# Second stage's first rows and query weights prepared in the last tiles of the first stage, on a new layout of buffers

## What is computed

```
# layer 0, and the attention of layer 1: cross attention over 77 context rows, 16 heads of 32
q, k, v = x @ Wq.T + bq, ctx @ Wk.T + bk, ctx @ Wv.T + bv
a = softmax((q k^T * tau + delta) / sqrt(32)); x = x + (a v) @ Wo.T + bo
# layer 0, feed forward on the normalized row
s = ln(x) @ Win + bin; x = x + (sum_h relu(s * W1 + b1) * W2 + b2) @ Wout + bout
# layer 1, feed forward: local attention over windows of 64 rows and both neighbours, 8 heads of 64
q, k, v = split(ln_w(x) @ Wqkv.T); light = softmax(q k_window^T / 8) v_window @ Wout_l.T
# and routing: 50 iterations on one score per row, top 256 / 512 rows of each sequence,
# dense attention among the chosen rows, scattered back
```

## Time and profile before

| | us |
|---|---|
| median of 3 runs (lowest, highest) | 3143.72 (3143.63, 3144.43) |
| the profiled execution's own time | 3161.28 |
| its span, first to last instruction | 3159.4 |
| mean granted TensorE clock | 0.975 of full speed |
| TensorE, VectorE, GpSimd, ScalarE busy | 2985.1, 2378.9, 1780.1, 1540.8 |

### The profile page before, as it was taken

One profiled execution on the slowest core, in us unless ns is written; L12 is line 12 of the kernel. 1 busy time (PEld: TensorE's weight loads), 2 busy tenths in 40 slices (PEclk: granted clock), 3 DMA queues, 4 the chain that ended last, 5 costly groups with the idle time before them and its releaser, 6 DMA issues.

```text
span 3159.4 us, 58477 instructions
## 1 busy us (share of the span) xinstructions
PE 2985.1 (94%) x24002; PEld 2324.6 (74%) x24002; DVE 2378.9 (75%) x3974; ACT 1540.8 (49%) x2349; POOL 1780.1 (56%) x1284
## 2 busy tenths in 40 slices
PE   7999999999999999999969999999999999979898
PEld 4777777777677777777747777777777777857776
DVE  4788888888888988888746767778878775566453
ACT  2566666666666666565433434333333333334343
POOL 1666565656558999999834545454455445573210
PEclk9999999999999999999979999999999999999999
DMA  4001010101112111111120111111222221131100
GB/s 161 34 30 54 28 56 29 55 34 55 46 54 83 51 57 51 54 41 41 64 84 27 57 54 59 59 56 53 66 91 87 74 77 61 47 134 54 34 18 11
DMA packets 87466, 180.42 MB, mean 57 GB/s; under 512 B 9526, under 2 KB 10294, under 8 KB 85664
## 3 DMA queue, kind: packets, MB, share of 16 engines
q1 hardware_dynamic: 82512, 161.73, 14.6%
q0 software_dynamic: 3968, 10.50, 1.1%
q10 hardware_dynamic: 720, 4.46, 0.3%
HBM read 106.05 MB, written 70.60 MB: 56 GB/s over the span
## 4 chain that ended last, share of the span: by engine, by line
PE 77%; DVE 11%; POOL 4%; issue 4%; ACT 3%; DMA 1%; POOLq 0%; SPq 0%; another core or an unknown queue 0%; DVEq 0%; ACTq 0%
PE ps L264 17%; PE ps L266 15%; PE ps L265 15%; PE ps L271 7%; PE ps L259 4%; PE ps L1129 4%; PE ps L479 3%; PE ps L491 3%; PE ps L1149 3%; PE ps L500 2%; PE ps L1723 2%; DVE Sb L636 1%; DVE sTa L616 1%; POOL sTa L842 1%; PE ps L1706 1%
## 5 line engine op out<-in xcount | busy, mean ns | idle before, releaser
L822 POOL TENSOR_TENSOR Sb<-Sb,mx 128x1232 f32<-128x1232 f32 x128 | 295.9, 2312 | 158.4 <-DVE mx L643 158.4
L827 POOL TENSOR_TENSOR Sb<-Sb,dn 128x1232 f32<-128x1232 f32 x128 | 288.6, 2254 | 155.9 <-DVE dn L651 155.7
L1536 POOL TENSOR_TENSOR Sw<-Sw,dw 128x1024 f32<-128x1024 f32 x128 | 242.3, 1894 | 233.1 <-DVE dw L1254 232.8
L1481 ACT COPY PU<-ps 128x512 f32<-128x512 f32 x256 | 141.1, 588 | 438.2 <-PE ps L271 437.2
L777 ACT COPY PT<-ps 77x1024 f32<-77x1024 f32 x256 | 256.8, 1003 | 181.3 <-PE ps L491 179.7
L1531 POOL TENSOR_TENSOR Sw<-Sw,mw 128x1024 f32<-128x1024 f32 x128 | 243.3, 1901 | 121.7 <-DVE mw L1247 121.6
L1241 DVE TENSOR_TENSOR Sw<-ps,msk 128x1024 f32<-128x1024 f32 x128 | 155.6, 1216 | 105.2 <-PE ps L1129 105.2
L271 PE MATMUL ps<-ident,xn 128*128 128x128 f32 x1120 | 176.0, 285 | 55.4 <-ACT xn L709 15.4
L264 PE MATMUL ps<-Wo,OTp 128*128 128x512 f32 x512 | 208.7, 408 | 19.5 <-DVE OTp L655 19.0
L636 DVE TENSOR_TENSOR Sb<-ps,dlt 128x616 f32<-128x616 f32 x256 | 198.3, 775 | 37.4 <-PE ps L479 37.3
L479 PE MATMUL ps<-KB,QT 64*128 64x154 f32 x2048 | 198.0, 314 | 26.1 <-DVE Sb L636 25.9
(11 more groups left out here) (276 smaller groups left out, 8135.0 us busy)
## 6 DMA issues: line engine op xcount, KB each, us to landing
XB<-in_x SPq DMA_DIRECT2D x16, 1024.0 KB, 5.5
x_scratch<-XB SPq DMA_DIRECT2D x16, 1024.0 KB, 4.4
XB<-x_scratch SPq DMA_DIRECT2D x16, 1024.0 KB, 5.7
x_scratch<-XB SPq DMA_DIRECT2D x64, 256.0 KB, 2.0
XL<-x_scratch SPq DMA_DIRECT2D x64, 256.0 KB, 3.0
XY<-x_scratch SPq DMA_DIRECT2D x64, 256.0 KB, 2.7
y_scratch<-XY SPq DMA_DIRECT2D x64, 256.0 KB, 2.0
out<-yo SPq DMA_DIRECT2D x64, 256.0 KB
```

The costliest lines, as they stand in the source:

```text
L822: G.tensor_tensor(sv, sv, last(mx[:, n % 2, :], NK), ALU.subtract).then_inc(g_sub, 1)
L827: G.tensor_tensor(sv, sv, last(dn[:, n % 2, :], NK), ALU.mult).then_inc(g_norm, 1)
L1536: G.tensor_tensor(weights(n, p), weights(n, p), last(dw[:, n % 2, 4 * p:4 * p + 4], 256), ALU.mult).then_inc(bg_norm, 1)
```

## The change

- **Layout.** Three arenas now outlive the stages. Wq moves into `arena_q`; the second stage's split query weights WlQ lie on it, and later XH, the gathered rows. XB moves into `arena_b`; on it lie QU, PU, XL (on the slot that unit 27 used, LASTB = 3) and Wlo[0], later xh and KH. On `arena_x`, beside raw, lie KU (on raw), route (on raw's last part), nulq, XY and yo. Wl becomes WlQ, WK and WV, each [128, 4, 512] in two halves.
- **Rows.** `early`, at place 12200 of the first stage, has SyncE load the first four tiles into XL once unit 27 is stored and scored; the four loads at the second stage's head go.
- **Raw weights.** `raws` loads three column parts (query, key, value; 1 MB each) on three semaphores in place of four row parts.
- **Query weights.** `wq`, at 12650, 12670, 12690, 12710, splits them in the first stage: four scaled copies on ScalarE, four fused subtractions on VectorE (128 x 512).
- **Second stage's head.** The split is twelve pieces of 128 x 512 at new places: key weights -306 to -297, value weights -296 to -287, output weights -266 to -257. The null query row is loaded by `loadn` at -150, after the value weights' split.
- **Waits.** Key copies (ScalarE) and the first routing step (VectorE) wait for the value weights' split. The gathers at the stage's end wait for the last query group (b_qk 124), no longer for the last key and value groups.

```diff
+LASTB = (2 * NB - 4) % 5
     yield 400 * (2 * NB - 1) + 100, "raws", ()
+    yield 400 * (2 * NB - 1) - 200, "early", ()
+    for k in range(4):
+        yield 400 * (2 * NB - 1) + 250 + 20 * k, "wq", (k,)
...
-    for k in range(8):
-        yield -300 + 3 * k, "wl", (k,)
+    for k in range(12):
+        yield -306 + (0, 10, 40)[k // 4] + 3 * (k % 4), "wl", (k,)
...
+    yield -150, "loadn", ()
...
-        QU, Sw = at("QU", 0, [128, 2, 4, D]), at("Sw", 4096, [128, 2, 2048])
+        KU, XY = at("KU", 0, [128, 2, 4, 640]), at("XY", 6144, [128, 3, D])
...
+        at_q, at_b = arena("arena_q", 4096), arena("arena_b", 10240)
+        Wq = [at_q(f"Wq{i}", 2048 * i, [128, 4, D], R) for i in (0, 1)]
+        WlQ = [at_q(f"Wlq{i}", 2048 * i, [128, 4, D], R) for i in (0, 1)]
+        XB = at_b("XB", 0, [128, 5, 4, D])
+        QU, PU = at_b("QU", 0, [128, 2, 4, D]), at_b("PU", 4096, [128, 16, 128])
+        XL = at_b("XL", 2048 * LASTB, [128, 4, D])
...
@@ first stage, VectorE
+            def wq(k):
+                ve.wait_ge(a_whi, 21 + k)
+                V.scalar_tensor_tensor(WlQ[1][:, k, :], raw[:, k, 0:D], lnwb[:, k:k + 1], WlQ[0][:, k, :].bitcast(F),
+                                       ALU.mult, ALU.subtract).then_inc(v_wlo, 1)
@@ first stage, ScalarE
+            def wq(k):
+                ac.wait_ge(pe_q, 8 * NB)
+                ac.wait_ge(ld_raw[0], 16)
+                ac.wait_ge(ld_small, 144)
+                A.mul(WlQ[0][:, k, :], raw[:, k, 0:D], lnwb[:, k:k + 1]).then_inc(a_whi, 1)
@@ first stage, SyncE
-                for k in range(4):
-                    SY.dma_start(raw[:, k, :], a["wqkv"][:, k, :]).then_inc(ld_raw, 16)
+                for p in range(3):
+                    SY.dma_start(raw[:, :, D * p:D * p + D], a["wqkv"][:, :, D * p:D * p + D]).then_inc(ld_raw[p], 16)
+
+            def early():
+                done_x(2 * NB - 5)
+                for n in range(4):
+                    SY.dma_start(XL[:, n, :], X3d[128 * n:128 * n + 128, :]).then_inc(ld_xl[n], 16)
...
@@ second stage, TensorE
-                pe.wait_ge(bv_wl, 4)
+                if k < 4:
+                    pe.wait_ge(v_wlo, 24)
+                else:
+                    pe.wait_ge(bv_wl, 4)
...
@@ second stage, VectorE (the split; ScalarE's half is cut in the same way)
             def wl(k):
                 ve.wait_ge(ba_wl, k + 1)
+                w, j = (WK, WV, Wlo)[k // 4], k % 4
+                if k < 8:
+                    q = slice(D * (k // 4 + 1), D * (k // 4 + 2))
+                    V.scalar_tensor_tensor(w[1][:, j, :], raw[:, j, q], lnwb[:, j:j + 1], w[0][:, j, :].bitcast(F),
+                                           ALU.mult, ALU.subtract).then_inc(bv_wl, 1)
...
@@ the gathers, GpSimd
             gp.wait_ge(bv_rt, 42)
-            gp.wait_ge(b_qk, 8 * NB)
-            gp.wait_ge(b_v, 68)
+            gp.wait_ge(b_qk, 8 * (NB - 1) + 4)
...
@@ key copies, ScalarE
                     c = k - 4
+                    ac.wait_ge(bv_wl, 8)
...
@@ second stage, SyncE
+            def loadn():
+                sy.wait_ge(bv_wl, 8)
+                SY.dma_start(nulq[:, :], a["nulq"]).then_inc(ld_nq, 16)
...
-            for n in range(4):
-                load_xl(n)
             SY.dma_start(wlo_raw, a["wlo"]).then_inc(ld_w2, 16)
             SY.dma_start(msk[:, :, :], a["c_mask"]).then_inc(ld_w2, 16)
-            SY.dma_start(nulq[:, :], a["nulq"]).then_inc(ld_w2, 16)
```

More of the change, by code:

```diff
@@ L308, in build @@
         vepsl, nm_, rs = sb("vepsl", [128, 2, 4]), sb("nm_", [128, 2, 4]), sb("rs", [128, 2, 4])
-        Wq = [sb(f"Wq{i}", [128, 4, D], R) for i in (0, 1)]
         Wo = [sb(f"Wo{i}", [128, 4, D], R) for i in (0, 1)]
@@ L522, in wbias @@
                     p = take("wbo")
+                    pe.wait_ge(ld_raw[2], 16)
                     pe.wait_ge(g_cf, 4)
@@ L969, in sync_a @@
             block(2)
-            walk_a(vals0=vals0, vals1=vals1, loadk=loadk, loadv=loadv, store=store, storeb=storeb, kv=kv, loadx=loadx, wlo=wlo, raws=raws)
+            walk_a(vals0=vals0, vals1=vals1, loadk=loadk, loadv=loadv, store=store, storeb=storeb, kv=kv, loadx=loadx, wlo=wlo, raws=raws, early=early)
             for i in range(4):
@@ L980, in build @@
         pa.close()
-        at = arena("arena_w", 12288)
-        Wl = [at(f"Wl{i}", 6144 * i, [128, 4, 3 * D], R) for i in (0, 1)]
+        at = arena("arena_w", 8192)
+        WK, WV = ([at(f"Wl{n}{i}", 2048 * i + o, [128, 4, D], R) for i in (0, 1)] for n, o in (("k", 0), ("v", 4096)))
         places = (("Wkv", 0, 2 * D), ("Wh", 4096, D), ("Who", 6144, D))
@@ L996, in build @@
         xU = [sb(f"xU{i}", [128, 4, 576], R) for i in (0, 1)]
-        Wlo = [sb(f"Wlo{i}", [128, 4, D], R) for i in (0, 1)]
+        Wlo = [at_b("Wlo0", 8192, [128, 4, D], R), sb("Wlo1", [128, 4, D], R)]
         msk = sb("msk", [128, 3, 256])
-        nulq = sb("nulq", [128, D])
-        XL = sb("XL", [128, 4, D])
-        XY = sb("XY", [128, 3, D])
-        KU = sb("KU", [128, 2, 4, 640])
+        nulq = at_x("nulq", 5632, [128, D])
+        Sw = sb("Sw", [128, 2, 2048])
         VU = sb("VU", [128, 10, D])
-        PU = sb("PU", [128, 16, 128])
         wlo_raw = PU[:, :, :].rearrange("p a b -> p (a b)").rearrange("p (k m) -> p k m", k=4)
         mw, dw = sb("mw", [128, 2, 8]), sb("dw", [128, 2, 8])
-        yo = sb("yo", [128, D])
-        rout = sb("route", [128, 4, 128])
+        yo = at_x("yo", 7680, [128, D])
+        rout = at_x("route", 5120, [128, 4, 128])
         sr, zr, er = rout[:, 0, :], rout[:, 1, :], rout[:, 2, :]
@@ L1114, in v @@
                 pe.wait_ge(bv_xlo, 4 * i + 4)
-                pe.wait_ge(bv_wl, 4)
+                pe.wait_ge(bv_wl, 8)
                 r = 128 if j < 4 else 64
                 q = slice(128 * j, 128 * j + r)
-                mms3(ps[0:r, p, :], [(xU[0][:, x, q], xU[1][:, x, q], Wl[0][:, x, 2 * D:3 * D],
-                                      Wl[1][:, x, 2 * D:3 * D]) for x in range(4)]).then_inc(b_v, 1)
+                mms3(ps[0:r, p, :], [(xU[0][:, x, q], xU[1][:, x, q], WV[0][:, x, :], WV[1][:, x, :])
+                                     for x in range(4)]).then_inc(b_v, 1)
             def scores(n, p):
@@ L1469, in wl @@
             def wl(k):
-                if k < 4:
-                    ac.wait_ge(ld_raw, 64)
-                    A.mul(Wl[0][:, k, :], raw[:, k, :], lnwb[:, k:k + 1]).then_inc(ba_wl, 1)
-                else:
-                    ac.wait_ge(ld_w2, 80)
-                    A.copy(Wlo[0][:, k - 4, :], wlo_raw[:, k - 4, :]).then_inc(ba_wl, 1)
+                w, j = (WK, WV, Wlo)[k // 4], k % 4
+                if k < 8:
+                    ac.wait_ge(ld_raw[k // 4 + 1], 16)
+                    q = slice(D * (k // 4 + 1), D * (k // 4 + 2))
+                    A.mul(w[0][:, j, :], raw[:, j, q], lnwb[:, j:j + 1]).then_inc(ba_wl, 1)
+                else:
+                    ac.wait_ge(ld_w2, 64)
+                    A.copy(w[0][:, j, :], wlo_raw[:, j, :]).then_inc(ba_wl, 1)
             def pcopy(n, q):
@@ L1614, in build @@
         yg = sb("yg", [128, 3, 2, D])
-        xh = [sb(f"xh{i}", [128, 4, 768], R) for i in (0, 1)]
-        QH, KH = sb("QH", [128, 2, 4, 256]), sb("KH", [128, 2, 4, 512])
+        xh = [at_b(f"xh{i}", 3072 * i, [128, 4, 768], R) for i in (0, 1)]
+        QH, KH = sb("QH", [128, 2, 4, 256]), at_b("KH", 6144, [128, 2, 4, 512])
         VH = sb("VH", [128, 2, 4, 8, 65])
```

44 lines of the change are left out of this document (21 added, 23 removed).

## The result

The changed kernel took 3130.41 us (median of 5 runs, 3124.34 to 3132.15) where the kernel before took 3143.82 in the same comparison (5 runs, 3143.63 to 3146.01): 13.4 us faster by the medians. The ratio of the means is 0.9952 [0.9938, 0.9967], 0.48% or 15 us. The forecast was 3135.5, the range 3132.5 to 3140.5: the direction was right, the gain larger than the range allowed. Two repeats in later comparisons gave 0.9969 [0.9957, 0.9980] and 0.9966 [0.9954, 0.9978]; the three, weighted by their intervals, give 0.9964, some 11 us.

The account below looks back on a forecast made before the run. TensorE was taken as the bound, busy 94% of the span, so only its standing stretches could give time. Head 7.15, gate 1.0 and last tiles 0 gave 3143.7 - 8.2 = 3135.5 us, 8-in-10 range 3132.5 to 3140.5.

Parts of the forecast that it names:

- Head of the second stage: Seam of first and second stage: first query matmul at 1626.5 instead of 1633.65 us, 9.7 us after the last reduction.
- The half microsecond for the memset: Second stage's head: GpSimd's edge clearing holds the first normalization, ending it at 1618.1 instead of 1617.5 us.
- the 7.15 us: Second stage's head: term 1, queries start 7.15 us earlier and the gain is carried on; between 5.0 and 7.65.
- the 1.7 us that I had put in play there: Second stage's first queries: the same first 4.4 us at 1.2 GHz assumed, with some 1.7 us in play.
- Rival 3: Second stage's queries: clock does not rise, nine more matmul groups at 1.2 GHz cost 18.4 us, time 3153.9; chance 0.03.
- Last tiles: End of first stage: query weights' split costs zero under TensorE's work; likely 4.1 us on VectorE against 9.5 idle.
- Gate: End of second stage: first gather starts at 2778.2 instead of 2781.03 us, gated by the last query group.
- term 2: End of second stage, GpSimd's chain: 1.0 us gained from the earlier gathers, between 0 and 2.8.
- 7.15 + 1.0 + 0 = 8.2: Whole kernel: second stage's head, gathers' gate and first stage's last tiles summed; 8.2 us subtracted from the 3143.7 us median.

Follow-up runs that it names:

- rep_after: The changed kernel run again with nothing altered; 3149.58 us, ratio 0.9969 to the kernel before.
- the hole: Third stage's last gather burst held until TensorE turned 25 half tiles: kernel before 3154.49 and 3150.47 us, changed kernel 3143.89 and 3136.91 us.
- gate_back: The changed kernel with only the gathers' gate as before (last key and value group in place of last query group); ratio 0.9980 to the kernel before.
- hole_after: The changed kernel with the third stage's last gather burst held until TensorE turned 25 half tiles; 3143.89 us, ratio 0.9955 to the kernel before.

## Why the prediction was right and wrong

**Head of the second stage: right, term by term.** Gap 9.09, 9.31 and 9.08 us in three profiles of the changed kernel (9.7 predicted), against 16.85 and 16.38. The rows' part was 3.5 us and the query split's 2.4, and the order's 1.5. The half microsecond for the memset was too much: three normalizations took 1.52 to 1.53 us, in rep_after 1.68, so it held them by 0.15 us at most. What VectorE showed in the earlier trace rows beside a 4160-wide memset does not carry over to two of 256.

**What the clock gave back.** I carried the 7.15 us to the end unchanged. From the last reduction to the stage's first output sum the kernel before takes 88.4 to 88.7 us (four profiles, those with the hole counted in, since it lies behind), the changed schedule 81.4 to 82.5 (six): 6.4, not 7.4. gate_back has the same head and took 79.9, so the six don't show the whole spread. The stretch between the first query matmul and that sum holds the difference: 12.6 to 13.0 us of it are at the lower clock in five of the six (9.8 in the first profile, 5.6 in gate_back) and 8.1 to 8.7 in the kernel before. The level rose 5.8 to 6.2 us into the queries in the five, 4.6 to 5.3 before; the greater part is a second fall, 44 us in, which lasted 6.8 us instead of 3.4. Of the 1.7 us that I had put in play there, 1 was lost, but mostly at a fall that I hadn't looked at. Rival 3 did not come: the level rose.

**Last tiles: right that they cost nothing.** The hold came (6.15 us for four, L628's sort), and VectorE's idle time took it: TensorE stood no longer than without it, 8.1 us. Doubled, 1.9 us showed. Here I named a rule of the Trainium skill, SBUF — State Buffer, Who interferes with whom, by which a VectorE instruction with two SBUF inputs contends with a GpSimd instruction that reads SBUF. The trace agrees: 2.10 us beside GpSimd's 2.25, 0.66 without. In five other profiles with the split in that place the four took 3.0 to 3.4 us, so the hold is a matter of where they fall.

**Gate: right in the first profile, mostly absent in the later ones.** 1.3 us at the subtraction, and 0.1 to 0.2 in the eight later profiles, since ScalarE's late start takes the wait's place: the lower bound of my term 2. Over the stretch from the 56th to the 64th output sum, nine profiles with the new gate took 115.8 to 116.7 us and nine with the old one 115.9 to 119.2, means 116.2 and 117.2: 1.0, but that is where the clock fell: all nine with the new gate have 3.4 us at the lower clock there, and the four old ones that also have 3.4 took 115.9 to 116.9. Whether the gate moves the clock is open.

**The step that failed** is the last one, the sum "7.15 + 1.0 + 0 = 8.2", subtracted from the median. Its terms came out near their size: by stretches, 6.4 us for the first and at most 1.1 for the second. What failed is that it puts everything outside the two seams at nothing, with 3 us of range below the forecast. By the medians the change brought 13.4, 10.0 and 11.1 us, and 10.6 and 13.6 with the hole in both kernels: each of the five is above 8.2. The whole gain, by the three comparisons without the hole, is 11 us with some 2.5 us either way, and by stretches (means of four profiles of before and six of the changed schedule) it is

```
to tile 120's output sum          0.9   (ranges overlap)
last tiles                        0.9   (ranges overlap)
last reduction to first sum       6.4
to the 56th sum                  -0.3
56th to 64th                      1.1
64th to the third stage's first
  output, first profile left out  0.9   (ranges overlap)
rest, the stretch of the load
  left out                        0.5
sum                              10.4
```

6.4 + 1.1 = 7.5 is what the change's own steps bring. The other 3 us are spread over stretches whose ranges overlap: to tile 120's sum the kernel before took 1533.4 to 1538.7 us and the changed schedule 1532.7 to 1535.7, though ahead of it only addresses and the four early row loads had changed (in all profiles of the new layout it is 1530.1 to 1538.0). Whether the 3 us are chance or a small effect of the addresses stays open. So does why the first pair stood at 13.4.

The stand in the third stage doesn't explain it. Two traces of one kernel differ by 13.3 us there and 5.3 ahead of it, and the kernel before was profiled with both. Had its runs of the first comparison had them, while the changed kernel's had not, the pair would have differed by some 26 us (7.5 + 18.6). It differed by 13.4, and the median of before was itself 17.56 us below its profile: its runs most likely had no such stand either, but none of them was profiled. That the profile stood so far above the median was a sign of this, and I named no cause for it.

## What to carry to other kernels

A stage's head that waits for transfers, splits and turns at once is worth taking apart into parts whose inputs exist earlier; the parts' gains in the gap added up here to within 0.2 us when each was put back alone. Before a difference of two profiles is read as a change's effect, profile the same kernel twice and compare stretch by stretch: a program of 24,000 matmuls has stretches that differ by 13 us with no edit at all. And where TensorE stands with "issue" ahead of it, look which engine stood first, and whether the instruction that TensorE is held at starts just behind another engine's end. Two events that are late together, here an instruction load and a stretch, are not yet cause and effect: count how far the engine had got when the event came.

## What the hardware showed that I had not expected

Beside a burst of 15 indirect transfers of GpSimd (912 packets, a third of the 16 queues' time in 25 us) ScalarE started a copy 1.4 to 5.8 us after its input was ready in 17 of 18 profiles, and 0.04 us after it in one; TensorE stood behind it. At the end of the second stage, beside the gathers under the new gate, ScalarE's half of the product started 1.1 to 1.2 us after TensorE's end in eight of nine profiles and 0.05 us after it in the same one, the first. The record doesn't show the cause.

TensorE's instruction load of 16 KB, 0.9 to 1.2 us long by itself in this stretch, came 10 to 12 us late beside the burst, but hardly later than TensorE itself (674 matmuls and weight loads on, against 672, in hole_after). The Trainium skill, Runtime: NRT & Kernel Launch, Instruction fetch mechanics, says that the cost of crossing a 16 KiB boundary of the instructions is mostly hidden. The traces agree, in this burst too: TensorE was busy for 15.90 of 15.90 us around the load of hole_after.
